# Between the scores of the last group: products and values in small parts

## The reference, cut to what matters

```python
Q, K, V = (proj(Wq), proj(Wk), proj(Wv))
O = _flash_attention(Q, K, V, BLOCK, scale)        # causal, softmax over the keys
x = _layernorm(x + einsum('btm,nm->btn', O, Wo))
# feed-forward: rows and weights rounded to 8-bit integers, one product, scaled back
lhs_scale = absmax(x, rows) / 127;  rhs_scale = absmax(rhs, columns) / 127
acc = int32 product of round(x / lhs_scale) and round(rhs / rhs_scale)
x = _layernorm(x + acc * lhs_scale * rhs_scale)
```

## Time and profile before

| | |
|---|---|
| median of 3 runs | 1014.88 us (1013.63 to 1015.7) |
| the profiled execution | 1012.61 us, of which its span is 1010.9 us |
| busy share of the span | PE 94%, DVE 79%, ACT 71%, POOL 27% |
| the chain that ended last | PE 75%, DVE 13%, ACT 9%, issue 2% |
| share of TensorE's clock granted in the profiled execution | 0.988 on the mean |

### The profile page before, as it was taken

The page is one execution under the profiler, slowest core; times in us unless marked ns, Lnnn a source line. Parts: engine busy times, 40 slices in busy tenths (PEclk is TensorE's granted clock), DMA queues, the critical chain, the costliest instruction groups (busy, mean ns, idle before and its releaser), DMA issues.

```text
span 1010.9 us, 36007 instructions
## 1 busy us (share of the span) xinstructions
PE 950.8 (94%) x15664; PEld 484.8 (48%) x15664; DVE 801.1 (79%) x1081; ACT 716.4 (71%) x1494; POOL 271.4 (27%) x443
## 2 busy tenths in 40 slices
PE   8989999999999999999999999999999999999993
PEld 5645545544544454445444554455545554443432
DVE  4488888887888788878878998999898999566426
ACT  3523458788778877887878877888778877766670
POOL 4433452102210221022213331242214211453322
PEclk9999999999999999999999999999999999999996
DMA  5555440002210221022301240123103204412101
GB/s 176 175 184 160 155 124 13 6 8 55 62 34 9 58 63 29 9 64 66 85 8 48 68 120 10 37 76 90 43 12 91 58 24 120 94 34 75 33 2 42
DMA packets 70846, 66.15 MB, mean 65 GB/s; under 512 B 14704, under 2 KB 65200, under 8 KB 70688
## 3 DMA queue, kind: packets, MB, share of 16 engines
q1 hardware_dynamic: 70688, 63.84, 22.5%
HBM read 42.43 MB, written 20.91 MB: 63 GB/s over the span
## 4 chain that ended last, share of the span: by engine, by line
PE 75%; DVE 13%; ACT 9%; issue 2%; DMA 0%; POOL 0%; POOLq 0%; DVEq 0%; SPq 0%; ACTq 0%
PE ps_acc L725 20%; PE ps_score L681 18%; PE ps_max L681 18%; DVE block_max L1043 9%; ACT PR L974 7%; PE ps_score L604 5%; PE ps_score L611 3%; PE ps_max L796 2%; PE ps_max L679 2%; PE ps_max L699 1%; PE ps_score L796 1%; ACT accS L964 1%; PE ps_acc L585 1%; PE ps_score L710 1%; DVE stats L1143 1%
## 5 line engine op out<-in xcount | busy, mean ns | idle before, releaser
L1043 DVE TENSOR_REDUCE block_max<-ps_max 128x2 f32<-128x1024 f32 (+3 forms) x640 | 653.8, 1060 | 121.0 <-PE ps_max L681 58.0
L974 ACT ACTIVATE PR<-ps_score 128x512 f32<-128x512 f32 (+3 forms) x1280 | 619.8, 542 | 154.7 <-PE ps_score L681 137.2
L681 PE MATMUL ps_score<-QS,KS 99*32 99x512 bf16 (+3 forms) x5120 | 424.1, 350 | 22.2 <-ACT PR L974 18.1
L681 PE MATMUL ps_max<-KS,QS 96*32 96x512 bf16 (+3 forms) x4544 | 328.5, 349 | 7.1 <-DVE block_max L1043 4.7
L725 PE MATMUL ps_acc<-PR,VG 128*32 128x512 f32 (+3 forms) x2560 | 297.2, 530 | 0.0
L681 PEld LDWEIGHTS ps_score<-QS,KS 99*32 99x32 bf16 x5120 | 153.8, 95 | 209.6 <-ACT PR L974 110.2
L681 PEld LDWEIGHTS ps_max<-KS,QS 96*32 96x32 bf16 x4544 | 128.9, 96 | 134.4 <-DVE block_max L1043 62.0
L1289 POOL TENSOR_SCALAR_AFFINE_SELECT PR<-PR 128x512 f32<-128x512 f32 x128 | 81.9, 640 | 281.5 <-ACT PR L974 281.4
L725 PEld LDWEIGHTS ps_acc<-PR,VG 128*32 128x32 f32 x2560 | 82.3, 110 | 29.4 <-issue 0.7
L699 PE MATMUL ps_max<-mask_q,ident_b 128*32 128x64 bf16 (+3 forms) x1808 | 95.7, 200 | 0.0
L1297 POOL CAST max_parts<-neg_max 16x128 bf16<-16x128 f32 (+1 forms) x30 | 9.1, 302 | 201.5 <-ACT neg_max L956 199.0
(11 more groups left out here) (125 smaller groups left out, 556.6 us busy)
## 6 DMA issues: line engine op xcount, KB each, us to landing
QS<-qparts SPq DMA_DIRECT2D x192, 64.0 KB, 2.4
KS<-kparts SPq DMA_DIRECT2D x192, 64.0 KB, 2.4
qparts<-end_slots SPq DMA_DIRECT2D x16, 384.0 KB, 3.7
kparts<-end_slots SPq DMA_DIRECT2D x16, 384.0 KB, 3.1
PR<-in_L_attn_x SPq DMA_DIRECT2D x8, 512.0 KB, 4.5
heads_out<-accS SPq DMA_DIRECT2D x112, 32.0 KB
end_slots<-in_L_attn_x SPq DMA_DIRECT2D x6, 512.0 KB, 7.5
out_y<-end_slots SPq DMA_DIRECT2D x12, 256.0 KB, 2.2
```

What stands on the lines that cost most here:

```text
L681: m = pe.matmul(bank[t * QW:t * QW + QW, 0:w], stack[:, t * QW:t * QW + QW], moving, start=True, stop=stop)
L974: act.activation(PR[:, k % 4, j, 0:w], ps_score[:, bank_of(use), 0:w], ACT.Exp, scale=SCALE).then_inc(s_exp, 1)
L1043: dve.tensor_reduce(block_max[:, h * PAIR:h * PAIR + PAIR, i, b], ps_max[:, slot_at:slot_at + PAIR, 0:w], AX.X, ALU.max).then_inc(s_reduce ...
```

## The change

Only PE's order in the last group changes; ACT, DVE, POOL and SP run the same instructions in the same order as before. A step of the last group now is: S0; first half (h = 0) of tile 0's projection; token sums and spread; turn; S1; second half of that projection (with `wo_last`); the values for the first half of their columns; S2; first half of tile 1's projection; product; S3; the second half of that projection; the values for the second half of their columns. The values of a step so become two sets of four matmuls with half as many columns each, 40 times. The waits of the values stand ahead of their first half, those of the projection ahead of its first half. The other seven groups and what follows step 39 keep their order.

```diff
                 def values(g, k):
-                    s = skip(c, kb)
+                    values_wait(g, k)
+                    values_of(k, skip(c, kb), CH).then_inc(s_pv, 1)
...
+                def values_half(g, k, h):
+                    s = skip(*STEPS[k])
+                    middle = s + (CH - s) // 2
+                    if h == 0:
+                        values_wait(g, k)
+                        values_of(k, s, middle)
+                    else:
+                        values_of(k, middle, CH).then_inc(s_pv, 1)
...
-                            if j % 2:
-                                project(NS * g + k, j // 2)
-                        end_parts(NS * g + k)
-                        if k >= LAG:
-                            values(g, k - LAG)
-                        elif g:
-                            values(g - 1, NS + k - LAG)
+                            if g == GROUPS - 1:
+                                between_scores(k, j)
+                        if g < GROUPS - 1:
+                            if k >= LAG:
+                                values(g, k - LAG)
+                            elif g:
+                                values(g - 1, NS + k - LAG)
...
+                def between_scores(k, j):
+                    at = NS * (GROUPS - 1) + k
+                    project(at, j // 2, j % 2)
+                    if j == 0:
+                        joins(at)
+                        late_turn(at)
+                    if j == 2:
+                        late_product(at)
+                    if j % 2:
+                        values_half(*divmod(at - LAG, NS), j // 2)
```

More of the change, by code:

```diff
@@ L715, in values, with values_wait @@
                     c, kb = STEPS[k]
-                    s = skip(c, kb)
+                    values_wait(g, k)
+                    values_of(k, skip(c, kb), CH).then_inc(s_pv, 1)
+                def values_wait(g, k):
+                    c, kb = STEPS[k]
                     pe.wait_ge(s_exp, score_use(g, k, HG - 1) + 1)
@@ L723, in values, with values_of @@
                         pe.wait_ge(s_vg, CHUNKS * g + c + 1)
+                def values_of(k, a, b):
+                    c, kb = STEPS[k]
+                    s = skip(c, kb)
                     for j in range(HG):
-                        m = pe.matmul(ps_acc[EYE * j:EYE * j + EYE, s:CH], VG[:, kb, j, :], PR[:, k % 4, j, 0:CH - s],
-                                      start=kb == 0, stop=k == LAST[c])
-                    m.then_inc(s_pv, 1)
+                        m = pe.matmul(ps_acc[EYE * j:EYE * j + EYE, a:b], VG[:, kb, j, :], PR[:, k % 4, j, a - s:b - s],
+                                      start=kb == 0 and a == 0, stop=k == LAST[c] and b == CH)
+                    return m
+                def values_half(g, k, h):
[6 more added lines that the diff above has]
+                        values_of(k, middle, CH).then_inc(s_pv, 1)
                 def group(g):
@@ L797, in tiled, with late_product @@
                     return y
-                def end_parts(k):
+                def late_product(k):
                     for e in late_due(k, "product"):
@@ L811, in end_parts, with late_turn @@
                         y.then_inc(e_prod, 1)
+                def late_turn(k):
                     for e in late_due(k, "turn"):
@@ L820, in end_parts, with joins @@
                         y.then_inc(e_turn, 1)
+                def joins(k):
                     for m in joins_due(k):
@@ L824, in end_parts, with project @@
                         spread_inverses(e)
-                    for e in due(k, "finish"):
-                        finish_projection(e)
-                def project(k, t):
+                def project(k, t, h):
                     for e in late_due(k, f"project{t}"):
                         m, s = divmod(e, 2)
-                        if t == 0:
+                        if t == 0 and h == 0:
                             pe.wait_ge(e_on, HALVES * (m + 1))
@@ L839, in project @@
                                 pe.wait_ge(e_last, LAST_STEPS * joined(m) + 3 + s)
-                        at = s * HALF + t * P
+                        at, n = s * HALF + t * P, half_rows(m, h)
                         rows = ps_max[:, s, t * D:t * D + D]
[L842 to L850, removed]
+                        if m == ENDS - 1:
+                            pe.matmul(rows, o_in(m)[0:n, h, at:at + P], wT[0:n, 3, h, :], start=t == 0 and h == 0, stop=False)
+                            continue
+                        last = h == HALVES - 1
+                        y = tiled(rows, o_in(m)[0:n, h, at:at + P], wT[0:n, 3, h, :], h == 0, last and m not in JOINED)
+                        if last and m in JOINED:
                             y = tiled(rows, accS[:, m % 2, at:at + P], wo_last[:, :], False, True)
-                        if m < ENDS - 1:
+                        if last:
                             y.then_inc(e_y, 1)
@@ L899, in _ @@
                     for t in range(TPH):
-                        project(k, t)
-                    end_parts(k)
+                        for h in range(HALVES):
+                            project(k, t, h)
+                    late_product(k)
+                    late_turn(k)
+                    joins(k)
+                    for e in due(k, "finish"):
+                        finish_projection(e)
             @block.scalar
```

## The result

| | before | after |
|---|---|---|
| median of 18 runs each | 1014.65 us | 1017.04 us (1015.97 to 1020.54) |
| ratio | | 1.0024, 95% interval 1.0016 to 1.0032 |
| profiled execution, its span | 1012.61, 1010.9 | 1018.56, 1016.8 |
| clock granted to TensorE, mean | 0.988 | 0.981 |

The change makes the kernel 2.4 us slower; forecast were 1017.6 and +2.7.

A forecast was written before the change was run, and what follows sets the result against it. PE bounds projection steps, ACT plain ones; the end hangs on step 10's fourth score and DVE's run to step 15's reciprocal. Sum 0.5 - 0.44 + 1.1 + 1.1 + 1.5 - 1.32 + 0.3 = +2.7, median 1017.6, range 1014.0 to 1020.4.

The forecast's parts named there:

- A plain step is ACT's at 2.14, and the order inside it is worth nothing: Plain steps: twelve exponentials in 6.42, 0.535 each, 2.14 a step against PE's 1.73; no gain put there.
- The halves cost 0: Values split in 40 steps: tails stay hidden, 0; if not, 0.21 on ten steps, 2.1.
- Steps 9, 17, 27, 29: Finer parts win 0.44 in each: -0.44 for step 9, -1.32 for steps 17, 27 and 29.
- Steps 2 to 8: Values of step 2 wait for POOL's mask, delaying accS and step 6's token sums: +0.5 at step 8's start.
- Step 10: More work ahead of its fourth score makes the mask, residual and start of DVE's run later: +1.1.
- Step 15 and the clock: Three scores and the product come after the spread's wait for DVE's reciprocal, +1.1; half clock behind it, +1.5.
- The turns: Waiting for integers idles ACT in steps 22, 24, 34, 36: 1.4, of which 1.1 made good, +0.3.
- Rival B: Last group: ACT fed evenly, DVE's run not later, step 15's spread not in PE's way: -2.5, 1012.4; chance 0.10.

The follow-up runs named there:

- the run with step 10 edited: Changed kernel, in step 10 alone the first half of tile 1's projection and the product behind S3: 1016.92 us, ratio 1.0021.
- the halves alone: Kernel before with only the values split in two halves, behind the second and fourth score: 1010.05 us, ratio 0.9951.
- the kernel with all joins late: Changed kernel with turns, token sums and spreads all put back behind the last scores and the product: 1011.45 us, ratio 0.9965.
- the filled wait: Changed kernel with 12 products that nothing reads put into PE's wait ahead of step 15's spread: 1016.39 us, ratio 1.0018.

## Why the prediction was right, and where it was not

The time and the sign came out by luck, on two errors of some 3 us that cancel. The gains were put at 1.76 (four steps at 0.44) and the costs at 4.5, of which 0.3 for the turns. The runs show a gain of 5.0 and, against that, costs of 7.4 (5.0 + 2.4), which the ratios divide as 1.4 for the smaller projections and the early product, 0.8 for sums and other spreads, 1.9 to 2.7 for the turns, 2.4 to 3.2 for the spread of step 15. The first two lie within the uncertainty of their own comparisons.

**"A plain step is ACT's at 2.14, and the order inside it is worth nothing"** is the step that failed most: it put at nothing what the halves win in plain steps. It divided 6.42 by 12. After, twelve take 5.99, and PE's plain step is 1.95 (timelines of after; the two rows of PE are halves of values a step apart):

```profile
967.14 0.61 PE L734 MATMUL ps_acc<-PR,VG 128*32 128x256 f32 x8
...
969.09 0.61 PE L734 MATMUL ps_acc<-PR,VG 128*32 128x256 f32 x8
...
966.26 5.99 ACT L1006 ACTIVATE PR<-ps_score 128x512 f32<-128x512 f32 x12 [1.19 <-PE ps_score L681]
```

The trace of before had the answer. That same burst in narrower views of the timeline (its first three exponentials, its fourth and fifth, its fifth and sixth), and PE beside it:

```profile
960.08 1.57 ACT L974 ACTIVATE PR<-ps_score 128x512 f32<-128x512 f32 x3 [1.78 <-PE ps_score L681]
...
961.52 1.33 ACT L974 ACTIVATE PR<-ps_score 128x512 f32<-128x512 f32 x2
...
962.26 1.08 ACT L974 ACTIVATE PR<-ps_score 128x512 f32<-128x512 f32 x2
...
960.73 0.40 PE L681 MATMUL ps_score<-QS,KS 99*32 99x512 bf16 x4 [0.26 <-ACT PR L974]
960.95 1.03 PE L725 MATMUL ps_acc<-PR,VG 128*32 128x512 f32 x8
961.82 0.82 PE L681 MATMUL ps_score<-QS,KS 99*32 99x512 bf16 x12
962.91 0.40 PE L681 MATMUL ps_score<-QS,KS 99*32 99x512 bf16 x4 [0.27 <-ACT PR L974]
```

PE's step is 2.18 there (960.73 to 962.91). Three exponentials take 1.57. A single one takes some 0.60, so each further one adds 0.485, and twelve should take 0.60 + 11 x 0.485 = 5.94, not 6.42. The missing 0.48 is two stops of some 0.25, one at each change of step inside the burst. Consecutive exponentials overlap, so the burst counts as busy throughout, but the starts show the stop: the fourth exponential starts at 961.52 and the fifth only at 962.26, 0.74 later. The fifth needs the first score behind the values: PE did 0.87 of values in one piece (960.95 to 961.82), and this score then takes 0.40 more, to 962.22. Three times 0.48 and one time 0.74 is PE's 2.18. With halves the stops are gone (the bursts of 5.99), and with whole values PE's waits are back. PE's own wait of 0.26 was seen, and taken for proof that ACT was the slower engine. Both engines were waiting for each other in turn. Four times 0.485 is 1.94, and 1.95 is the step that came out. Two figures of the Trainium skill fit the shorter time: one element a cycle at 1.2 GHz (ScalarE: Activation LUTs, section What ACT_TABLE_LOAD costs) is an estimated 0.427 for 512 columns, and with its 51 ns of overhead on PSUM (Perfetto Trace Analysis, section Optimizing Scalar/DVE Operations) 0.478. The short burst's 0.485 agrees with that, the 0.535 does not.

**The halves cost 0**: right. A half takes 0.43 to the next start (967.14 to 967.57 of the timeline after), two as much as a whole. The estimate from the Trainium skill's load time (TensorE: Matmul & The Clock Gate, section LDWEIGHTS) would have been 8.5 us more; the loads are hidden, as the 0.62 for a set had said.

**Steps 9, 17, 27, 29**: 0.44 each in the trace, as put: 2.41, 2.62, 2.17 and 2.17 us long. **Steps 2 to 8**: the wait for the mask is there, 0.94. The shift at step 8 is 2.07, not 0.5, in a trace where half clock lasted 6.8 us; the run with step 10 edited, whose steps 2 to 8 are in the same order, had no such stretch at all, so it is not the order alone that makes it. Why the profiled execution lies above its median stays open: the fastest of the 18 had the same mean clock, 0.981.

**Step 10**: its last exponential came 1.13 later against the step's start, forecast 1.1, and DVE's run with it. That this belongs into the sum was wrong: two runs that undo it gain nothing that can be measured.

**Step 15 and the clock**: 1.1 + 1.5 = 2.6 was forecast; the move costs 2.4, 3.2 and 3.5 in three comparisons. The mechanism stands (no late reciprocal, no loss), and the clock was 0.50 when the spread started. In the trace the half clock lasted 6.8 us and not 3.0. (The stretch at 904 to 907, with 1.91 of 3.00 us busy, was fuller than this wait, and not thinner as the prediction has it.) How the price divides between wait and clock stays open.

**The turns**: 1.4 gross, of which 1.1 was to be made good and 0.3 to stay. What reaches the end is 1.75. An idle of 0.34 in the trace is more than 0.34 lost: the exponential behind the turn of step 34 starts 1.08 after the one before it (972.51 to 973.59), 0.59 more than the pace of 0.485. And the reserve, ACT's wait of 0.71 at step 38, is not there with halves: with the turns put back ACT's timeline has no idle time in steps 31 to 38 (964.32 to 981.27), so most of what a turn holds up comes later at the end. From step 29 to the end, with the clock full in all of them, it is 34.87 before, 32.74 with the halves alone, 33.77 after and 32.61 with the turns put back: the halves win 2.13, the early turns take 1.16 of it back, and the rest of what was moved costs nothing there.

**Rival B** was turned down on the right ground (the spread stands in PE's way), but its price, 2.5, missed the plain steps; the mechanism that it names is worth twice that.

## What to carry to other kernels

When two engines hand work back and forth through few buffers, get the rate of each from its shortest undisturbed burst and not from a long busy one: the difference between the two is the stop that a busy row hides, the starts of neighbours show where it lies, and smaller pieces on the other engine win it. Split work that fills; leave work that waits (a spread for an inverse, a turn for its integers, a sum for a copy) behind the pieces that feed the other engine. And a change of many parts can hide a gain behind a loss: here one of its parts alone makes 5.0 us out of a change that costs 2.4.

## What the chip showed that was not expected

The granted clock's falls moved about with small edits. Up to the spread of the end, the last group's PE stood at half clock for 3.4 us in the kernel with all joins late (907 to 911), for some 17 in after, and for some 17 in the kernel with the turns put back, which is 2.7 us faster than after all the same. In that kernel the clock stayed at half through 2.00 us in which PE did nothing, and through 5 us of full work behind them; its windows:

```profile
912.00:914.00 2.00, 0.00 (x0) 0.00 (x0) 1.90 (x5) 0.30 (x1) 0.72 (x1) 0.50 0.00 0
914.00:919.00 5.00, 4.98 (x64) 2.96 (x68) 1.95 (x5) 2.06 (x4) 0.34 (x1) 0.50 0.16 52
```

Edits of a microsecond at one place were cancelled in the trace by a fall at another (step 10, the filled wait). A single trace could not price them; only the medians could.
